# Rows of a gated attention layer: moved by indirect transfers through DRAM in place of products with matrices of zeros and ones, in a four-layer hybrid block on one core

## What is computed

```python
x = x + attn_a(layernorm(x))   # l=0: causal attention, 16 heads of 16, rotary positions
x = x + gated(layernorm(x))    # l=1
x = x + attn_b(layernorm(x))   # l=2: attention, 16 heads of 64, with a relative bias
x = x + gated(layernorm(x))    # l=3, same weights as l=1

def gated(t):                                   # B=8, N=512, D=256, C=256
    gate = sigmoid((t @ Wg)[..., 0])            # one number for each row
    _, idx = top_k(gate, C)                     # the 256 rows with the highest gates
    a = take_along_axis(t, idx[..., None], 1)   # those rows, ordered by gate
    o = attention(a @ Wq, a @ Wk, a @ Wv) @ Wo  # 16 heads of 16, 256 x 256 scores
    out = zeros_like(t)
    return out.at[batch, idx].set(o * gate[idx])  # back to their places, scaled; the rest is zero
```

## Time and profile before

| | |
|---|---|
| three runs | 2162.10, 2163.89, 2167.36 us; median 2163.89 |
| profiled execution | 2163.86 us, of which its span 2162.1 us |
| TensorE busy, matrix products | 2077.1 us, 96% of the span, 14694 instructions |
| VectorE busy | 1438.5 us, 67% |
| ScalarE busy | 1094.0 us, 51% |
| GpSimd busy | 562.8 us, 26% |
| DMA | 98.56 MB, mean 46 GB/s; share of the 16 engines' span 13.8% |

### The profile page before, as it was taken

One profiled execution on the slowest core, in us unless ns is written; L12 is line 12 of the kernel. 1 busy time (PEld: TensorE's weight loads), 2 busy tenths in 40 slices (PEclk: granted clock), 3 DMA queues, 4 the chain that ended last, 5 costly groups with the idle time before them and its releaser, 6 DMA issues.

```text
span 2162.1 us, 38720 instructions
## 1 busy us (share of the span) xinstructions
PE 2077.1 (96%) x14694; PEld 1276.1 (59%) x14694; DVE 1438.5 (67%) x4530; ACT 1094.0 (51%) x2465; POOL 562.8 (26%) x785
## 2 busy tenths in 40 slices
PE   7889999999999999999999999999999999999997
PEld 4456566654666555764566645766456664666665
DVE  8876554667756776567656587575875767756435
ACT  2344573646536474363744646346563646526552
POOL 4311231243212331133311332114230233202220
PEclk9999999999999999999999999999999999999999
DMA  3001121121111110121101111011110121101200
GB/s 139 2 1 40 42 90 40 54 74 33 43 40 54 57 42 27 40 72 47 39 22 57 62 40 42 18 57 62 40 59 1 57 69 50 43 16 57 68 18 10
DMA packets 29047, 98.56 MB, mean 46 GB/s; under 512 B 2880, under 2 KB 11200, under 8 KB 28736
## 3 DMA queue, kind: packets, MB, share of 16 engines
q1 hardware_dynamic: 28864, 96.09, 13.3%
HBM read 91.89 MB, written 4.19 MB: 44 GB/s over the span
## 4 chain that ended last, share of the span: by engine, by line
PE 86%; DVE 7%; ACT 5%; issue 1%; POOL 1%; DMA 0%; SPq 0%; DVEq 0%; POOLq 0%; ACTq 0%
PE ps L845 25%; PE ps L1498 11%; PE ps L1508 11%; PE ps L1490 10%; PE ps L1283 10%; PE ps L1340 4%; PE ps L1429 3%; PE ps L1360 3%; PE ps L1374 3%; PE ps L1460 2%; PE ps L1448 2%; ACT PTc L1029 2%; DVE ps L1148 2%; DVE mcol L1224 1%; ACT probs L1061 1%; DVE probs L1241 1%
## 5 line engine op out<-in xcount | busy, mean ns | idle before, releaser
L993 POOL TENSOR_SCALAR probs<-probs,rtotal 128x512 f32<-128x512 f32 x512 | 345.1, 697 | 1022.5 <-DVE rtotal L1250 1021.4
L1061 ACT ACTIVATE probs<-probs,peak 128x512 f32<-128x512 f32 x512 | 365.2, 714 | 238.8 <-DVE peak L1246 238.7
L1241 DVE CUSTOM_DVE_ANT_0 probs<-ps,band 128x512 f32<-128x512 f32 x512 | 332.8, 687 | 134.1 <-PE ps L1490 133.8
L1070 ACT ACTIVATE PT<-ps 128x512 f32<-128x512 f32 x512 | 263.7, 612 | 74.4 <-PE ps L1498 72.8
L1148 DVE CUSTOM_DVE_ANT_0 ps<-ps,later 128x128 f32<-128x128 f32 (+3 forms) x512 | 233.1, 525 | 39.7 <-PE ps L1340 38.8
L1498 PEld LDWEIGHTS ps<-ident,probs 128*128 128x128 f32 x2048 | 224.0, 141 | 47.5 <-issue 31.5
L1498 PE MATMUL ps<-ident,probs 128*128 128x128 f32 x2048 | 250.1, 275 | 0.5 <-POOL probs L993 0.2
L1490 PE MATMUL ps<-KT,QT 64*128 64x512 f32 x1024 | 249.0, 611 | 0.0
L1508 PE MATMUL ps<-PT,Vb 128*64 128x512 f32 x1024 | 235.4, 599 | 0.5 <-ACT PT L1070 0.5
L845 PE MATMUL ps<-xnT,wb 128*128 128x512 f32 x512 | 234.6, 597 | 0.8 <-ACT xnT L1012 0.3
L1029 ACT ACTIVATE PTc<-ps 128x384 f32<-128x384 f32 (+1 forms) x384 | 166.3, 543 | 69.6 <-PE ps L1360 69.6
(11 more groups left out here) (125 smaller groups left out, 2808.5 us busy)
## 6 DMA issues: line engine op xcount, KB each, us to landing
band<-in_band SPq DMA_DIRECT2D x64, 896.0 KB, 4.5
wb<-in_w_b SPq DMA_DIRECT2D x64, 384.0 KB, 3.1
x<-in_x SPq DMA_DIRECT2D x16, 256.0 KB, 3.0
out<-x SPq DMA_DIRECT2D x16, 256.0 KB, 2.3
wob<-in_wo_b SPq DMA_DIRECT2D x1, 1024.0 KB, 8.3
wqk<-in_wqk_a SPq DMA_DIRECT2D x1, 512.0 KB, 5.6
cos_t<-in_cos SPq DMA_DIRECT2D x1, 256.0 KB, 5.4
sin_t<-in_sin SPq DMA_DIRECT2D x1, 256.0 KB, 6.0
```

Source lines behind the costliest of these rows:

```text
L993: last = g.tensor_scalar(unit, unit, rtotal[:, r % 8, e:e + 1], 1.0, ALU.mult, ALU.mult)
L1061: last = a.activation(unit, unit, ACT.Exp, bias=peak[:, r % 8, e:e + 1], accum_out=total[:, r % 8, e:e + 1])
L1070: a.activation(PT[:, k % 2, e, :, tile_of(q)], bank(now, name).rearrange("p (k n) -> p k n", k=NT), ACT.Copy).then_inc(act_read, 1)
L1241: v.tensor_tensor_reduce(out=probs[:, r % ROWS_HELD, e, :], in0=bank(now, name), in1=band[:, k % 2, e, lo:lo + T], scale=1.0, scalar=-3e38 ...
```

## The change

The slot of each row becomes an unsigned integer and is used as an address. Two tensors in DRAM for each of the two places of memory, `ranked` and `results` (512 rows each), hold the rows.

- New step `f_send`, after `f_rank`: GpSimd issues four indirect DMAs, each of which writes 128 rows of xn to their slots in `ranked`; SyncE waits for all four and loads slots 0 to 255 to `xg`. `f_gather` is now four transposes of `xg`.
- `f_spread`, `pick`, `spread_t` and their constants go.
- After `f_o` SyncE stores `of` to slots 0 to 255 of `results`. New step `f_back`: GpSimd waits for that store and issues four indirect DMAs, each of which reads 128 rows from `results` by their slots into `yt`. Slots 256 to 511 were set to zero once at the start.
- `f_y` has no product any more: VectorE multiplies `yt` by the gate, adds x, and forms the moments as before, once all four transfers have landed.
- A gated layer has a buffer `xnf` of its own, so it no longer takes part in the holding of xn.
- WORK has new costs, the waits SENT, STORED and BACK (5.0, 2.6, 2.2 us) enter the planner, and all of PLACE is replaced, so the order of all steps changes.

```diff
-CONSTS = 8
+CONSTS = 5
-    "f_row": [("o", "dve", 1)], "f_rank": [("o", "dve", 1)], "f_spread": [("o", "dve", 1)], "f_gather": [("o", "act", 1)],
+    "f_row": [("o", "dve", 1)], "f_rank": [("o", "dve", 1)], "f_gather": [("o", "act", 1)],
-    "f_va": [("o", "dve", 1)], "f_vb": [("o", "dve", 1)], "f_o": [("o", "act", 1)], "f_y": [("o", "dve", 1)],
+    "f_va": [("o", "dve", 1)], "f_vb": [("o", "dve", 1)], "f_o": [("o", "act", 1)],
...
+    "f_rank": [("pe", 0.505), ("dve", 0.15)],
+    "f_gather": [("pe", 0.436), ("act", 0.48)],
...
-    "f_y": [("pe", 1.727), ("dve", 1.82)],
+    "f_y": [("dve2", 0.36), ("dve2", 0.36), ("dve", 1.14)],
...
+    "f_send": [("pool", 1.2), ("pool", 1.2), ("pool", 1.2), ("pool", 1.2)],
+    "f_back": [("pool", 1.2), ("pool", 1.2), ("pool", 1.2), ("pool", 1.2)],
...
-STORE_LOAD, FETCH, COLUMNS, CHOICE = 6.5, 5.0, 4.0, 1.0
+STORE_LOAD, FETCH, COLUMNS, SENT, STORED, BACK = 6.5, 5.0, 4.0, 5.0, 2.6, 2.2
...
-           (f("spread"), [f("rank")], []), (f("gather"), [f("rank")], [])]
+           (f("send"), [f("rank")], []), (f("gather"), [f("send")], [])]
...
-    out += [(f("o"), [f("vb", 0), f("vb", 1)], []), (f("y", 0), [f("o"), f("spread")], []), (f("y", 1), [f("o")], [f("y", 0)])]
+    out += [(f("o"), [f("vb", 0), f("vb", 1)], []), (f("back"), [f("o")], []), (f("y", 0), [f("back")], []),
+            (f("y", 1), [f("back")], [f("y", 0)])]
...
+        ranked = [nc.dram_tensor(f"ranked{i}", (T, D), F32, kind="Internal").ap() for i in range(2)]
+        results = [nc.dram_tensor(f"results{i}", (T, D), F32, kind="Internal").ap() for i in range(2)]
```

SyncE's side:

```diff
+                        if kind == "f_send":
+                            i = place_of(s, l)
+                            sp.wait_ge(rows_sent[i], 16 * NT * gated_turns[s, l])
+                            sp.dma_start(m.xg[:], ranked[i][0:CAP].rearrange("(j p) d -> p j d", p=P)).then_inc(rows_chosen[i], 16)
+                        if kind == "f_o":
+                            i = place_of(s, l)
+                            sp.wait_ge(act_read, plan.unit(now, now))
+                            at_least(sp, results_back[i], 16 * NT * (gated_turns[s, l] - 1))
+                            sp.dma_start(results[i][0:CAP].rearrange("(j p) d -> p j d", p=P),
+                                         m.of[:]).then_inc(results_stored[i], 16)
```

GpSimd's side:

```diff
+                        if kind == "f_send":
+                            i = place_of(s, l)
+                            pool.wait_ge(xn_done, plan.after("xn", Step("f_ln", s, l), now))
+                            pool.wait_ge(dve_read, plan.unit(Step("f_rank", s, l), now))
+                            at_least(pool, rows_chosen[i], 16 * (gated_turns[s, l] - 1))
+                            for t in range(NT):
+                                g.indirect_dma_start(ranked[i], bass.IndirectOffsetOnAxis(m.rank[:, t:t + 1], 0), m.xnf[:, t, :],
+                                                     None).then_inc(rows_sent[i], 16)
+                        if kind == "f_back":
+                            i = place_of(s, l)
+                            at_least(pool, zeroed, 32)
+                            pool.wait_ge(results_stored[i], 16 * gated_turns[s, l])
+                            for t in range(NT):
+                                g.indirect_dma_start(m.yt[:, t, :], None, results[i],
+                                                     bass.IndirectOffsetOnAxis(m.rank[:, t:t + 1], 0)).then_inc(results_back[i], 16)
```

VectorE's side:

```diff
+                        if kind == "f_y":
+                            i = place_of(s, l)
+                            dve.wait_ge(results_back[i], 16 * NT * gated_turns[s, l])
+                            for t in range(2 * n, 2 * n + 2):
+                                last = v.scalar_tensor_tensor(out=x[:, s % 2, t, :], in0=m.yt[:, t, :], scalar=m.gate[:, t:t + 1],
+                                                              in1=x[:, s % 2, t, :], op0=ALU.mult, op1=ALU.add)
+                            last.then_inc(added_done, 1)
...
                         if kind == "f_rank":
                             v.tensor_copy(m.rank[:], bank(now)[:, 0:NT]).then_inc(dve_read, 1)
-                            dve.wait_ge(dve_read, plan.unit(now, now))
-                            for t in range(NT):
-                                last = v.tensor_scalar(m.pick[:, t, :], slot_row[:], m.rank[:, t:t + 1], None, ALU.is_equal)
-                            last.then_inc(pick_done, 1)
-                        if kind == "f_spread":
-                            for j in range(NS):
-                                last = v.scalar_tensor_tensor(out=m.spread_t[:, j, :], in0=bank(now),
-                                                              scalar=slot_col[:, j:j + 1], in1=m.gate_row[:],
-                                                              op0=ALU.is_equal, op1=ALU.mult)
-                            last.then_inc(dve_read, 1)
```

TensorE's side:

```diff
                         if kind == "f_gather":
-                            pe.wait_ge(pick_done, plan.after("pick", Step("f_rank", s, l), now))
+                            i = place_of(s, l)
+                            pe.wait_ge(rows_chosen[i], 16 * gated_turns[s, l])
                             room(now)
                             for c in range(NC):
-                                last = product(o[:, c * CAP:(c + 1) * CAP], [(xn[:, t, tile_of(c)], m.pick[:, t, :])
-                                                                             for t in range(NT)])
+                                for j in range(NS):
+                                    last = te.transpose(o[:, c * CAP + j * P:c * CAP + (j + 1) * P], m.xg[:, j, tile_of(c)],
+                                                        ident[:])
...
-                        if kind == "f_y":
-                            read(now, Step("f_o", s, l))
-                            at_least(pe, dve_read, plan.unit(Step("f_spread", s, l), now))
-                            room(now)
-                            last = sums(o, lambda j, g: (m.spread_t[:, g, tile_of(2 * n + j)], m.of[:, g, :]), NS)
```

More of the change, by code:

```diff
@@ L36 @@
 Causal = namedtuple("Causal", "Qz K1 PTc xnTc mcol Vx rsums")
-Gated = namedtuple("Gated", "Qzf K1f PTf pick logit_junk gate_row above tie turnedf scaledf OTf spread_t xgT of mcolf Vxf rsums z "
-                   "gate rank")
+Gated = namedtuple("Gated", "xnf Qzf K1f PTf xg logit_junk gate_row above tie turnedf scaledf OTf yt xgT of mcolf Vxf rsums z gate "
+                   "rank")
 UNITS = {
@@ L66 @@
     "above": {"f_row": 1},
-    "pick": {"f_rank": 1},
+    "added": {"f_y": 1},
     "swirl": {"c_q": 1, "c_k": 1},
@@ L171, in wait_for @@
         return COLUMNS
-    if x.kind == "f_spread" and y.kind == "f_rank":
-        return -CHOICE
+    if x.kind == "f_gather":
+        return SENT
+    if x.kind in ("f_back", "f_y"):
+        return STORED if x.kind == "f_back" else BACK
     return FETCH if x.kind == y.kind == "b_row" else 0
@@ new lines @@
+    ("cycle", "f_q"): [2298],
+    ("cycle", "f_rank"): [2225],
+    ("cycle", "f_row"): [2452],
+    ("cycle", "f_send"): [2466],
+    ("cycle", "f_v"): [2326],
+    ("cycle", "f_va"): [2576, 2594],
+    ("cycle", "f_vb"): [190, 2536],
+    ("cycle", "f_y"): [2847, 2566],
+    ("cycle3", "f_back"): [6697],
+    ("cycle3", "f_gate"): [5081],
+    ("cycle3", "f_gather"): [6161],
+    ("cycle3", "f_k"): [6203],
+    ("cycle3", "f_ln"): [2538],
+    ("cycle3", "f_m"): [6546, 6770],
+    ("cycle3", "f_o"): [6866],
@@ new lines @@
+    ("first0", "f_back"): [4674],
+    ("first0", "f_gate"): [1578],
+    ("first0", "f_gather"): [4488],
+    ("first0", "f_k"): [4596],
+    ("first0", "f_ln"): [3938],
+    ("first0", "f_m"): [4906, 5106],
+    ("first0", "f_o"): [5948],
+    ("first0", "f_p1"): [1886, 4869, 3162, 1747],
+    ("first0", "f_p2"): [1736, 1685, 3277, 5363],
+    ("first0", "f_q"): [4706],
+    ("first0", "f_rank"): [3418],
+    ("first0", "f_row"): [1713],
+    ("first0", "f_send"): [3772],
+    ("first0", "f_v"): [5107],
@@ new lines @@
+    ("last1", "f_gather"): [36116],
+    ("last1", "f_k"): [33292],
+    ("last1", "f_ln"): [46386],
+    ("last1", "f_m"): [38466, 42609],
+    ("last1", "f_o"): [36938],
+    ("last1", "f_p1"): [35076, 37142, 37320, 41587],
+    ("last1", "f_p2"): [41980, 42584, 39978, 42122],
+    ("last1", "f_q"): [34601],
+    ("last1", "f_rank"): [34710],
+    ("last1", "f_row"): [37396],
+    ("last1", "f_send"): [34994],
+    ("last1", "f_v"): [35039],
+    ("last1", "f_va"): [42938, 42939],
+    ("last1", "f_vb"): [42295, 35468],
@@ new lines @@
+    ("last1", "f_y"): [38716, 41891],
+    ("last2", "f_back"): [36601],
+    ("last2", "f_gate"): [21930],
+    ("last2", "f_gather"): [24355],
+    ("last2", "f_k"): [25252],
+    ("last2", "f_ln"): [22839],
+    ("last2", "f_m"): [29699, 31954],
+    ("last2", "f_o"): [36601],
+    ("last2", "f_p1"): [25719, 28244, 29336, 23344],
+    ("last2", "f_p2"): [29621, 25466, 33119, 25166],
```

(19 more changed lines are left out.)

382 lines of the change are left out of this document (161 added, 221 removed).

## The result

The changed kernel takes 2202.14 us (median of three runs, 2197.22 to 2210.52) against 2163.89: ratio 1.0177, 95% interval 1.0161 to 1.0194. It is slower by 38 us, and the forecast was 2102. Its own runs lie 13 us apart, and so a smaller difference of a kernel that ran once says little.

What follows compares the result with a forecast made beforehand. TensorE's queue was taken to bound the middle, chain length both ends. Middle -80, end +13 and start +5 gave -62 us, so 2163.9 - 62 = 2102 us; forecast band 2085 to 2120, range 2068 to 2145.

Steps and rivals of the forecast that it cites:

- the middle: Seven repeating periods: TensorE loses 13.9 us of work each, 2.4 given back, period 261.5 to 250: -80 us.
- So that costs nothing: SyncE's queue: waiting about 7 us for four sends delays no band or weight loads, issued 65 us ahead: 0 us.
- No clock is to be won: TensorE, whole run: granted clock 0.996, already at the upper level of 2.4 GHz, so no gain.
- The end: Last gated layer, standing alone: both ways through DRAM lengthen its chain, +13 us.
- The start: First gated layer, beside causal work of sequence 1: bounds -7 and +13, taken as +5 us.
- c: GpSimd's time for one indirect DMA issue, eight a layer: taken as 1.2 us, upper end 2.6.
- rivals 3 and 4: 3: side strand sets the period, 2199 us, chance 0.10. 4: VectorE and GpSimd lock, 2617 us, chance 0.02.
- Rivals 1 and 2: Middle layers, TensorE idle. 1: 3.5 us each, 2133 us, chance 0.19. 2: 5.6 us, no change, 2164 us, 0.04.
- Nothing in the profile asks for just this size: Argument against no change (2164 us, chance 0.04), which needs 5.6 us more TensorE idle time per middle layer.
- I am wrong if the period is over 256 us with waits of the gather: Sign against the forecast in the middle: period over 256 us, waits at the gather or following layer's first transposes.

Runs made afterwards that it cites:

- no transfers, searched order: Changed kernel without the gated layers' DRAM transfers (rows neither chosen nor returned), PLACE searched anew with transfer times set to nothing: 2095.89 us.
- no transfers: Changed kernel in its own order, without the gated layers' DRAM transfers; transposes read xnf, additions read of: 2150.17 us.
- searched order, band waits: Changed kernel, PLACE searched anew with measured transfer times, GpSimd issuing xg's load and the results' store, SyncE holding the band's load until xg landed: 2158.48 us.
- the first experiment: Kernel before, own order; the gated layers' two product groups cut down to transposes, rows neither chosen nor returned: 2116.46 us beside 2166.93.
- run 5b: Changed kernel, own order; in SyncE's queue only band loads up to 14 places ahead of the send move behind xg's load: 2169.96 us (1.0029).

## Why the prediction was wrong, point by point

**The step that failed** is the middle, -80 us: "I give 2.4 us of the 13.9 back for that and take a period of 250". It was 263.3, and all 13.9 and 1.8 more were given back. Of the 100 us between forecast and result 67 lie in the five periods and 28 in the stretch to the last layer (the forecast's two other periods laid to the stretches on either side). TensorE's share of one period, from the windows of the five:

| kernel, us | period | busy | idle | fillers (number) | f_k and f_q |
|---|---|---|---|---|---|
| before | 261.5 | 255.5 | 6.0 | 13 | 7.75 |
| no transfers, searched order | 252.5 | 243.7 | 8.8 | 26 | 9.5 |
| no transfers | 259.5 | 247.9 | 11.6 | 55 | 7.8 |
| band's load behind xg's | 259.6 | 248.2 | 11.4 | 55 | 7.8 |
| after | 263.3 | 249.8 | 13.5 | 55 | 9.3 |
| searched order, band waits | 258.1 | 246.2 | 11.8 | 34 | 7.8 |

From 247.6 upward:
- 4.9 us (to 252.5) stay lost with no trips and an order searched for that case. TensorE's own share isn't had in full; the first experiment says the same (5.3 of 11.2). 1.8 of them are the lower clock: f_k and f_q take 9.5 us there instead of 7.75, with no transfer to wait for. The rest is idle time and fillers. Where before f_rank's count followed on 4.6 us of biased products without a gap, in the changed kernel (second block) and in the one without trips in its searched order (third) stand 20 fillers (2.35 us) and a wait of 1.8 us for the comparisons:

```profile
557.46 1.13 PE L1490 MATMUL ps<-KT,QT 64*128 64x512 f32 x4
558.52 3.65 PE L1508 MATMUL ps<-PT,Vb 128*64 128x512 f32 x16
562.10 0.18 PE L845 MATMUL ps<-ones,tie 128*128 128x1 bf16 x1
```

```profile
554.49 0.60 PE L1434 MATMUL ps<-ident,gate 128*128 128x128 f32 x4
554.92 2.35 PE L1349 MATMUL ps<-ident 128*128 128x128 f32 x20
559.02 0.18 PE L864 MATMUL ps<-ones,tie 128*128 128x1 bf16 x1 [1.75 <-DVE above L1251]
```

```profile
801.48 2.35 PE L1307 MATMUL ps<-ident 128*128 128x128 f32 x20
805.64 0.18 PE L848 MATMUL ps<-ones,tie 128*128 128x1 bf16 x1 [1.81 <-DVE above L1209]
```

 With TensorE at 98% the view of windows let a microsecond of its work look like one of time, while the chain of work that ended last had VectorE and ScalarE in it for 12% of its length already. My reading is that the two strands interlock, so that relief of one resource exposes the other's steps; no run takes that apart.
- 7.0 us (to 259.5) are the order that came with the change against one searched without trips: 29 more fillers, which are 3.9 us, and 2.8 us more of idle time. That it is the trips' length that asks for such room, and not only a poorer search, is what 258.1 (searched, with trips) against 252.5 (searched, without) says: 5.6 us a period. As f_k and f_q run at full speed in the former and not in the latter, the trips' part is rather larger.
- 0.1 us (to 259.6): the transfers themselves, once the order has room and nothing disturbs them.
- 3.7 us (to 263.3): the band's load, 2.1 of it in waits and 1.6 in f_k and f_q at the lower clock.

**"So that costs nothing"**, of SyncE's queue, was wrong in both ways. The prediction looked at whether band and weights would be late for their own users, never at the small urgent transfer among them. And the slack of the weights is not 65 us: moved by at most 14 places they were late by 47 us in the run.

**"No clock is to be won"** was right and was the wrong question. I never asked whether some could be lost. The mean went from 0.996 to 0.982. f_k and f_q of all layers take 14.9 us more (77.0 against 62.1).

**The end** was +13, and is +16.2 in the tail. The two trips measured 10.9 and 10.8 us, against the 10.8 and 11.7 worked out; they lengthen the chain by 12.2, and f_k and f_q at the lower clock add 2.6 (6.44 against 3.88): 14.8 of the 16.2. What was missed lies ahead of it: the stretch from the last full period to the last layer grew by 16.1. There one transpose group waits 5.8 us for `xg`, which meets the band too: with the band's load behind, the stretch is longer by 5.2 only. The tail itself varies: runs with the same two trips have it at +12.4 to +16.3.

**The start** was +5. With one of the seven periods laid to the stretch to 562 us the forecast for that stretch was -6.5, and it is -3.1. **c** was right (1.27 for 1.2), and that rules out rivals 3 and 4 by their own prices. Of the 96 distances between the issues of a burst one is 3.18 us (1966.61 to 1969.79, and as long at the same place in run 5b), the others are at most 1.52. What held that one up is open; once in a run it costs far less than either rival needs. The tally of sizes was good, then; the coupling was not.

**The rivals.** Rivals 1 and 2 had the mechanism (TensorE idle in another place) and stopped at 5.6 us a layer. 2202 would need about 8.4 ((38 + 97 - 18) / 14), and "Nothing in the profile asks for just this size" took the absence of a reason for a bound. The slower side was tied to one price, c; it came by the order and the queue instead. Of the signs named, "I am wrong if the period is over 256 us with waits of the gather" was the one that showed.

**What the change is worth.** Compared at the best orders found, 2158.5 against 2143.8, it costs 15 us. By the profiled spans, 17.4: +4.6 at the start, -6.0 in five periods (258.1 against 259.3), +2.9 to the last layer and +15.9 in the tail, where nothing covers the trips. Whether the last layer alone should keep its products was not tried.

## What to carry to other kernels

When work moves from a busy engine into a chain with latency, price three things apart: how much of the relief arrives when the products are simply cut (here half), what room the order must make for the latency (here 5.6 us a period), and the tail, where nothing hides it (12 to 16 us). Then look at what leaves on any queue within a few microseconds of each new small load: a large prefetch that isn't urgent belongs behind it in the same queue. And price an idle gap of some 2 us on TensorE at up to two and a half times its length: here 2.1 us of waiting were followed by up to 3.1 us more for the products behind it, at the lower clock.

## What the hardware showed beyond what was expected

- An indirect DMA of 128 rows of 1 KB keeps GpSimd 0.95 to 0.97 us (the first of four 1.06 to 1.13), the next starts 1.27 us after it, and it lands 2.4 us (to DRAM) or 2.8 us (from DRAM) after issue. VectorE wasn't held up by it: its commonest operation, `probs<-ps,band` (x512), has a mean of 688 ns, before 687.
- Two transfers in one queue go in their order (xg's load takes 3.0 us with 896 KB issued 0.42 us behind it, 4.9 us with them 0.38 us ahead). In two queues they share: 4.8 us even with the band 0.50 us behind. With it 1.25 us behind, xg landed after 3.1 us in four of five cases, as with no band near.
- Waits of 2.1 and 0.7 us around four transposes were enough for the clock to drop to 1.2 GHz, with f_k and f_q 1.7 to 3.1 us longer, but not each time: of the six first layers of the middle, with waits alike within 0.4 us, four show it. Nor is a transfer needed: without any, behind the wait of 1.81 us shown above and two shorter ones (0.35 and 0.69 us), they are 1.7 us longer (5.61).
